# A routing plan on VectorE, made in three parts over three pairs of steps in place of one

## What is computed

```
h = layernorm(x) * (1 + ca) + sa
x = x + ga * attention(h)
h = layernorm(x) * (1 + cb) + sb
top_w, top_i = top_k(h @ router_weight, 2)
x = x + gb * sum over the two experts of top_w * expert(h)
```

## Time and profile before

| | |
|---|---|
| median of 3 runs | 1631.35 us (1631.22 to 1633.74) |
| the profiled execution | 1640.98 us, span 1639.2 us |
| mean granted TensorE clock | 0.956 of full |
| busy in the span: PE, DVE, ACT, POOL | 84%, 82%, 67%, 59% |
| plans | 8, the first at 259.3 us, the last at 1487.4 us |

### The profile page before, as it was taken

One profiled execution on the slowest core, in us unless ns is written; L12 is line 12 of the kernel. 1 busy time (PEld: TensorE's weight loads), 2 busy tenths in 40 slices (PEclk: granted clock), 3 DMA queues, 4 the chain that ended last, 5 costly groups with the idle time before them and its releaser, 6 DMA issues.

```text
span 1639.2 us, 45619 instructions
## 1 busy us (share of the span) xinstructions
PE 1369.4 (84%) x14418; PEld 837.7 (51%) x14418; DVE 1336.8 (82%) x3943; ACT 1104.1 (67%) x2594; POOL 974.1 (59%) x1371
## 2 busy tenths in 40 slices
PE   2688888888888888888899888998889887888883
PEld 1244444455555454555456555655556554555662
DVE  5688999888988897888988898898987986665784
ACT  1388887777776776766677776777777755556452
POOL 1223335833585777667775777847775678277535
PEclk9999999999999998998999999999999998899996
DMA  3767676566677776677577767676777785668752
GB/s 101 168 161 159 154 159 150 146 151 162 167 195 175 179 175 164 172 182 166 148 188 179 168 164 170 168 188 162 172 195 173 197 196 143 156 178 227 204 160 64
DMA packets 436856, 274.13 MB, mean 167 GB/s; under 512 B 32684, under 2 KB 426446, under 8 KB 436622
## 3 DMA queue, kind: packets, MB, share of 16 engines
q1 hardware_dynamic: 402542, 230.30, 58.3%
q0 software_dynamic: 15360, 31.49, 6.9%
q10 hardware_dynamic: 18720, 9.44, 2.1%
HBM read 165.99 MB, written 105.04 MB: 165 GB/s over the span
## 4 chain that ended last, share of the span: by engine, by line
PE 31%; DVE 23%; POOL 17%; issue 14%; DMA 6%; ACT 4%; SPq 4%; POOLq 0%; ACTq 0%; DVEq 0%
DVE mx L1831 10%; PE ps_job L1195 6%; POOL slot_dram L770 5%; PE ps_s L1360 4%; POOL y_in L787 4%; DMA k_stk<-part_dram 3%; PE ps_q L1166 3%; PE ps_q L1182 2%; PE ps_q L1149 2%; PE ps_job L1294 2%; PE ps_st L1366 1%; POOL ln_rs L736 1%; PE ps_job L1216 1%; ACT prob L964 1%; DMA h_blk<-slot_dram 1%
## 5 line engine op out<-in xcount | busy, mean ns | idle before, releaser
L1831 DVE TENSOR_REDUCE mx<-ps_s 128x2 f32<-128x512 f32 x1024 | 655.4, 682 | 121.2 <-PE ps_s L1360 117.3
L964 ACT ACTIVATE prob<-ps_st 128x512 f32<-128x512 f32 x1024 | 558.5, 596 | 66.5 <-PE ps_st L1366 61.3
L1360 PE MATMUL ps_s<-k_stk,q_stk 51*128 51x256 bf16 x2048 | 360.3, 282 | 118.8 <-ACT prob L964 48.7
L1366 PE MATMUL ps_st<-q_stk,k_stk 53*128 53x256 bf16 x2048 | 355.4, 280 | 5.5 <-ACT prob L964 5.0
L1195 PE MATMUL ps_job<-prob,v_ext 128*32 128x256 f32 x4096 | 289.2, 401 | 24.8 <-issue 10.6
L1360 PEld LDWEIGHTS ps_s<-k_stk,q_stk 51*128 51x128 bf16 x2048 | 141.7, 96 | 315.9 <-DVE mx L1831 179.3
L770 POOL DMA_INDIRECT slot_dram<-h_row,slot x240 | 240.5, 1002 | 61.8 <-issue 60.2
L787 POOL DMA_INDIRECT y_in<-y_dram,slot x216 | 213.8, 990 | 65.3 <-issue 47.3
L908 ACT ACTIVATE o_sb<-ps_job 128x256 f32<-128x256 f32 x256 | 97.3, 380 | 176.2 <-PE ps_job L1195 171.7
L1195 PEld LDWEIGHTS ps_job<-prob,v_ext 128*32 128x32 f32 x4096 | 115.6, 112 | 128.3 <-issue 39.9
L809 POOL TENSOR_TENSOR qk_rest<-qk_f,qk_part 128x512 f32<-128x512 f32 x64 | 74.8, 1169 | 155.1 <-ACT qk_part L997 154.9
(11 more groups left out here) (229 smaller groups left out, 2701.5 us busy)
## 6 DMA issues: line engine op xcount, KB each, us to landing
w_q<-in_we SPq DMA_DIRECT2D x360, 128.0 KB
part_dram<-qk_part SPq DMA_DIRECT2D x128, 192.0 KB
q_stk<-part_dram SPq DMA_DIRECT2D x128, 192.0 KB
k_stk<-part_dram SPq DMA_DIRECT2D x128, 192.0 KB
h_blk<-slot_dram SPq DMA_DIRECT2D x46, 512.0 KB
y_dram<-y_sb SPq DMA_DIRECT2D x46, 512.0 KB
part_dram<-qk_part SPq DMA_DIRECT2D x128, 128.0 KB
mod_in<-row_dram SPq DMA_DIRECT2D x64, 192.0 KB
```

Source lines behind the costliest of these rows:

```text
L964: sc.activation(prob[:, (k ^ 1) % 8, :], ps_st[k % 2][:], ACT.Exp).then_inc(exp_done, 1)
L1360: mm = pe.matmul(ps_s[j % 2][:, t * S:(t + 1) * S], q_stk[us.tri][r0:r0 + R_BIAS, hp, t * P:(t + 1) * P], k_stk[us.tri][r0:r0 + R_BIAS, hp ...
L1366: mm = pe.matmul(ps_st[k % 2][:, t * S:(t + 1) * S], k_stk[ut.tri][r1:r1 + R_MAX, hp, t * P:(t + 1) * P], q_stk[ut.tri][r1:r1 + R_MAX, hp, ...
L1831: dve.tensor_reduce(mx[:, hp // 4, :, 4 * par + hp % 4], ps_s[j % 2][:].rearrange("p (t s) -> p t s", s=S), AX_X, ALU.max).then_inc(max_do ...
```

## The change

`plan(u)` becomes three functions. `plan_blocks` (L1708, L1710) stays at step 88, `plan_owners` (L1712 to L1726) goes to step 90, `plan_slots` (L1730 to L1736) to step 92, each at the place in `rest` where the plan stood. The instructions, their operands and semaphores are the same; `plan_slots` has one wait more, for the `owner` instruction.

```diff
-            def plan(u):
+            def plan_blocks(u):
...
                 dve.tensor_reduce(blocks[:], more, AX_X, ALU.add).then_inc(plan_step, 1)
+
+            def plan_owners(u):
+
+                c, n_blocks = u.group * PLAN, BLOCKS[u.group]
                 dve.wait_ge(plan_step, c + 2)
...
+
+            def plan_slots(u):
+
+                c, n_rows = u.group * PLAN, SIZES[u.group] * TT * 2
+                mine, rows = hot_start[:, 0:n_rows, :], start_of[:, 0:n_rows]
+                dve.wait_ge(plan_step, c + 7)
                 dve.wait_ge(rank_step, u.count(2, 2))
...
-                u = at(step, 88)
-                if u and u.last:
-                    plan(u)
+                for after, part in ((88, plan_blocks), (90, plan_owners), (92, plan_slots)):
+                    u = at(step, after)
+                    if u and u.last:
+                        part(u)
```

More of the change, by code:

```diff
@@ L1695, in take_rank @@
                    .then_inc(rank_step, 1)
-            def plan(u):
+            def plan_blocks(u):
                 c = u.group * PLAN
-                n_blocks, n_rows = BLOCKS[u.group], SIZES[u.group] * TT * 2
-                mine, rows = hot_start[:, 0:n_rows, :], start_of[:, 0:n_rows]
                 if u.group:
```

## The result

The changed kernel took 1677.21 us (median of 4 runs, 1668.91 to 1681.31), the kernel before on the same chip 1632.55 (4 runs, 1631.22 to 1644.96): ratio 1.0237, 95% interval 1.0194 to 1.0279, which is 31.7 to 45.5 us slower, 38.7 in the middle (the two medians are 44.7 apart). The forecast of slower by POOL's queue came true; the size did not, since +23 was predicted and 1664 us was the top of the range. The profiled execution took 1681.31 us, 40.3 more than that of before.

A forecast was written before the change was run, and what follows sets the result against it. No engine alone was taken as the bound; POOL's queue from first scatter to `act` was on the path. Per-group delays summed to +23.1 us, taking the median from 1631.35 to 1654 us, range 1628 to 1664.

The forecast's parts named there:

- slower by POOL's queue: Late slots delay POOL's first scatter and all queued behind it up to `act`: 15 us and more slower, chance 0.52.
- the sum: Per-group delays over all eight plans, -1.7 + 3.0 + 4.9 + 4.8 + 5.4 + 2.2 + 4.5 + 0, gave +23.1 us.
- the lower clock: TensorE's later stand may lower its granted clock: some 2 us more in each of groups 1 and 3, outside the sum.
- a gain for group 0: At group 0's plan, 2.0 us of VectorE waiting saved, less 0.3 for the router: -1.7 us.
- nothing for group 7: Planned after the last maxima, `att_tmp` earlier and the scatter a little later: taken as 0, between -1.7 and +1.7 us.
- The slots' time: When the moved slots end at each plan; for group 4, `att_tmp` at 989.81 as before plus 7.1 gave 996.9.
- POOL stands, and `act` and L1178 follow: POOL idle before the first scatters of groups 1 to 6, 3 to 5 us each, some 28 in all; `act` and L1178 equally late.
- Groups 1 to 4: Slots later than POOL's arrival at the first scatter by 3.0, 4.9, 4.8 and 5.4 us, each counted as lost time.
- POOL's delay as hidden: In group 5 only VectorE's lateness counts: about 2.0 us more idle and 0.2 for gaps, 2.2 us.
- counted whole at 4.5: In group 6 `act` is on VectorE, but POOL's gathers, which ScalarE waits for, run late: all 4.5 us counted.
- The hold-up by POOL's `x` addition: POOL's 0.72 us addition may hold up the owners on VectorE: up to 0.5 us at each of seven plans, 3.5 in all.
- The rule of the Trainium skill: Two-SBUF-input VectorE and SBUF-reading GpSimd instructions exclude each other; slots meet nobody, owners meeting the addition make it up to +26.6 us.

The follow-up runs named there:

- POOL's stand alone: Kernel before, with POOL's first scatter of groups 0 to 6 also waiting for the maxima of step 95: 1.0105 on a slower chip, 1.0280 on a faster one.
- slots first: Changed kernel with blocks, running sums and slots at step 88, only owners at step 90; against the kernel before: 1.0021 on a slower chip, 1.0028 on a faster one.
- Experiments 1 to 3: Kernel before with POOL's first scatter held, 1.0105 and 1.0280; changed kernel with slots at step 88, owners at 90, 1.0021 and 1.0028; with both at 90, 1.0094.
- experiment 2: Changed kernel with the slots made at step 88 and only the owners at step 90; against the kernel before: 1.0021 and 1.0028.
- experiment 6: The split made for group 0 alone, 1.0013 against the kernel before; for groups 1 to 7 only, 1.0221 beside the whole change's 1.0238.

## Why the prediction was wrong in size

The step that failed is the sum: it let a late scatter cost only the time by which the slots miss POOL, with the lower clock outside the sum, and it booked a gain for group 0 and nothing for group 7. This is where the time went, from plan to plan (us, single traces, all on the faster chips):

| stretch | before | changed | changed, second trace | POOL's stand alone | slots first | forecast for the change |
|---|---|---|---|---|---|---|
| start to plan 0 | 259.3 | 260.1 | 261.1 | 258.9 | 258.9 | - |
| plan 0 to 1 | 165.1 | 171.2 | 168.9 | 172.3 | 165.3 | -1.7 |
| plan 1 to 5 | 746.6 | 771.8 | 768.1 | 772.6 | 739.2 | +18.1 |
| plan 5 to 6 | 141.4 | 144.9 | 148.3 | 145.9 | 144.0 | +2.2 |
| plan 6 to 7 | 175.1 | 175.2 | 176.3 | 175.8 | 172.1 | +4.5 |
| plan 7 to the end | 151.8 | 156.4 | 152.1 | 155.9 | 153.9 | 0 |

The column of POOL's stand alone lies within 1.2 us of the change's in every stretch. By the prediction's own steps:

- **The slots' time.** Right for groups 1, 2, 3 and 6, within 0.4 us. For group 4 it was 1.9 too late, because I left `att_tmp` at its old distance, "since the router sets it". It came 4.4 us after the plan's start and not 6.0: with the lump gone, TensorE reached the router sooner. For groups 1 to 3 I had counted from the router's end itself, which held. VectorE's idle time there was 1.14 us, released by L1260 as predicted, and 1.09 before the maxima, not 2 to 3 in one place.
- **POOL stands, and `act` and L1178 follow.** Right, place for place: a stand of 5.34 us in group 4, L1178 there 4.3 us later after the plan's start, and waits for `act` 18.2 us up in all (20.5 in the second trace); for groups 1 to 4 I had counted 18.1. Experiments 1 to 3 show the held scatter to be the cause.
- **Groups 1 to 4, 18.1 us forecast, 25.2 measured (21.5 in the second trace).** This is the term that was sized too small. Their scatters were 19.2 us late and not 18.1. The start of a scatter that POOL stood for was missing, 0.77 us from the slots' end in each of the four, 3.1 us; that it shows so little is luck, since group 4's 1.9 offsets it. The lower clock, which I had named as an upper end of 2 us in groups 1 and 3 only, came in about so: 2.1 us in group 1, 0.9 in group 3, 0.5 in group 4, none in group 2. These 3.5 us belonged in the sum. Some 2 to 3 us of the 25.2 stay unexplained.
- **Group 5, "POOL's delay as hidden".** Its scatter was 4.7 us late and its stretch 3.5 us longer, against 2.2 forecast. The wait of 0.92 us that I took for it is group 4's; group 5's `att_tmp` waited for nothing before, and 0.95 us after.
- **Group 6, counted whole at 4.5.** Its scatter was 5.2 us late, but its stretch grew by 0.1 and 1.2 us. Here the rest of the kernel took most of the delay.
- **The hold-up by POOL's `x` addition** did show, inside the slots' times, though by the addition in groups 1 and 6 and by the subtraction L809 in groups 0 and 2 to 5, which each ended 0.28 us before L1714. L1714 took 0.55 to 0.89 us in all eight plans where it took 0.42 before, and L1719 0.28 in five of them where it took 0.17: 2.8 us in all, within the 3.5 that the prediction set as the bound. In group 1:

```profile
436.59 0.73 POOL L799 TENSOR_TENSOR x<-x,att_tmp 128x256 f32<-128x256 f32 x1
```

```profile
436.72 0.89 DVE L1714 TENSOR_TENSOR hot_start<-blocks,upto 128x256 f32<-128x256 f32 x1
```

  The rule of the Trainium skill ("SBUF — State Buffer", section Who interferes with whom) let the slots made under POOL's stand go free, and the trace agrees: L1744 took 0.19. The same section names `tensor_scalar` among the operations that can contend with GpSimd, and the 0.74 us of `over` in experiment 2 agree.
- **Group 0 and group 7.** Group 0 gave back nothing that could be seen. The slots' last instruction took 0.19 us there as forecast, but VectorE now waited 2.25 us for scores before the maxima of step 90 and 0.41 before `att_tmp`. Its stretch was 6.1 and 3.8 us longer, of which 5.7 can be chance (experiment 6). Group 7's first scatter was 3.0 us later; the tail behind it grew by 4.6 us in one trace and 0.3 in the other, and by 4.1 with POOL's stand alone, where group 7's scatter was not held, so its lateness does not explain the tail.

So the mechanism was right, and no addition of single terms gives the 39 us cleanly: stretches between two plans differ by several us from trace to trace (plan 2 to plan 3 was 188.4 before, 191.1 after, 180.9 in the slots-first kernel). The excess over the forecast is seen in groups 1 to 4 and around groups 0 and 7; its split there is open beyond the clock's 3.5 us and the scatters' start.

**Open.** Why the same stands cost less on the slower chips. There POOL's stand alone cost 18.5 us, although L1178's waits for `act` rose from 20.2 us in the kernel before (some 16 were expected) to 46.4, nearly as much as on the faster chip (15.8 to 46.8), where it cost 45.9. The mean granted clock may be part of it. As medians of the runs within one comparison it fell by little on the slower chips (0.928 to 0.921 with the change, 0.928 to 0.924 with POOL's stand) and by more on the faster ones (0.960 to 0.948, 0.961 to 0.944; 0.951 with the stands filled). That is argued, not shown. The slower chips' traces have something else that the faster ones' lack: waits of ScalarE and VectorE for which the view finds no instruction of this core ("remote"), in the unchanged kernel too,

```profile
ACT prob L964 <- remote: 55.0, 25, 5.7
```

135 us on ScalarE and 84 on VectorE in all in that trace, and none in the traces of the faster chips that were read for it. Part of POOL's stand may be hidden under them; what they are was not found. Open too is what carries the 20 us of scatters that start four steps later.

## What to carry to other kernels

When a step is moved, look up who needs its result first and how much slack there is between the two: here the result had 2.8 to 3.8 us before an in-order queue reached its reader, the move took 6.2 to 8.3 (groups 1 to 6), and everything in that queue came late. Split a long lump so that the part that others wait for is made first; the split with the slots first cost 0.2 to 0.3%, the one with the slots last 1.6 to 2.4%. And once a forecast says that TensorE will stand for 3 us, price the slower matmuls behind the stand in the sum and not as an upper end, but only where the same matmuls do not run at the lower clock already.

## What the runs showed of the hardware

- A scatter that POOL stood for starts 0.76 to 0.77 us after the end of the slots' instruction in every group from 1 to 7 of the changed kernel, and 0.31 us after it in group 0; one that finds its slots ready starts 0.15 to 0.19 us after the instruction before it.
- After stands of 2.8 to 3.2 us TensorE's matmuls took 0.74 us for four where they take 0.44 at the higher clock, in groups 1 to 4 of both traces of the changed kernel. A short stand does not rule this out: after 0.64 us they took 0.44 in group 1 of the kernel before, and after 0.58 us 0.74 in its group 4. With nine matmuls without use in the stand all four groups were at 0.44.
- A VectorE instruction that began 0.13 us after a POOL addition of 0.73 us took 0.89 us where it takes 0.42 alone.
- Chips differ by 8% in this same program: the unmodified kernel took 1633 to 1638 us in three comparisons and 1761 to 1776 in three others, with mean granted clocks of 0.956 and 0.921 in the two traces. The cost of one and the same edit differs with them (1.0105 against 1.0280), so here a ratio carried over from one chip to another in sign rather than in size.
